# A decoder block's expert tiles go from 256 rows (15 tiles) to 128 rows (23 tiles)

## The reference

```python
gate_weights = softmax(x @ Wg + bg)            # 8 experts
topv, topi = top_k(gate_weights, 2)            # each token takes 2 of them
h = gelu(x @ W1[e] + b1[e])                    # 256 -> 512
h = gelu(h @ W2[e] + b2[e])                    # 512 -> 512
y = h @ W3[e] + b3[e]                          # 512 -> 256
out = sum over the token's two experts of topv * y
```

## Time and profile before

| | |
|---|---|
| time, median of 3 runs | 884.95 us (883.24 to 885.09) |
| span of the profiled execution | 896.7 us |
| mean granted TensorE clock | 0.855 of full speed |
| PE busy | 671.8 us (75%) |
| DVE busy | 527.2 us (59%) |
| ACT busy | 344.6 us (38%) |
| POOL busy | 317.1 us (35%) |

### The profile page before, as it was taken

One profiled execution on the slowest core, in us unless ns is written; L12 is line 12 of the kernel. 1 busy time (PEld: TensorE's weight loads), 2 busy tenths in 40 slices (PEclk: granted clock), 3 DMA queues, 4 the chain that ended last, 5 costly groups with the idle time before them and its releaser, 6 DMA issues.

```text
span 896.7 us, 12741 instructions
## 1 busy us (share of the span) xinstructions
PE 671.8 (75%) x3876; PEld 471.4 (53%) x3878; DVE 527.2 (59%) x1035; ACT 344.6 (38%) x967; POOL 317.1 (35%) x271
## 2 busy tenths in 40 slices
PE   4729895341999999955799999998867574977465
PEld 3327442330788888954535555566545353555233
DVE  4885999664455555515314434355587858467785
ACT  2403301422333333322335455466445241544544
POOL 2450587554000000024078465471156928110000
PEclk9959998555999999985599999999989766687787
DMA  9740002556411111144000000000120000000000
GB/s 332 261 141 0 1 0 94 168 176 209 107 48 47 47 47 47 37 121 144 1 0 1 1 0 0 0 0 1 52 89 0 1 0 1 0 0 0 0 18 29
DMA packets 35713, 49.81 MB, mean 56 GB/s; under 512 B 3032, under 2 KB 26784, under 8 KB 35424
## 3 DMA queue, kind: packets, MB, share of 16 engines
q1 hardware_dynamic: 33152, 41.26, 14.5%
q0 software_dynamic: 2528, 8.13, 2.5%
HBM read 38.37 MB, written 11.01 MB: 55 GB/s over the span
## 4 chain that ended last, share of the span: by engine, by line
PE 60%; DVE 20%; ACT 8%; issue 5%; POOL 3%; DMA 2%; another core or an unknown queue 1%; SPq 0%; DVEq 0%; ACTq 0%; POOLq 0%
PE bank L1500 13%; PE bank L1513 4%; PE bank L1617 4%; PE bank L1616 3%; PE bank L1671 3%; PE bank L1803 3%; POOL sorted_rows L469 3%; PE bank L1638 2%; PE bank L1821 2%; ACT sm L689 2%; PE bank L1388 2%; DVE qk L902 2%; PE bank L1431 2%; PE bank L1432 2%; ACT s5m L773 2%
## 5 line engine op out<-in xcount | busy, mean ns | idle before, releaser
L644 ACT ACTIVATE hf<-bank,be 128x256 f32<-128x256 f32 x120 | 50.5, 472 | 86.3 <-PE bank L1500 72.3
L1500 PE MATMUL bank<-h,wsp 128*128 128x256 f16 x720 | 81.3, 273 | 2.1 <-DVE h L1054 1.4
L475 POOL DMA_INDIRECT yg<-expert_rows,pos x16 | 15.6, 975 | 185.7 <-DMA expert_rows<-yb 181.1
L1500 PEld LDWEIGHTS bank<-h,wsp 128*128 x720 | 69.6, 98 | 12.0 <-issue 3.8
L773 ACT ACTIVATE s5m<-bank,n 128x128 f32<-128x128 f32 x128 | 45.4, 370 | 75.4 <-DVE n L1252 75.3
L1052 DVE CAST h<-hf 128x512 f16<-128x512 f32 x60 | 25.6, 427 | 65.1 <-ACT hf L644 63.6
L1803 PE MATMUL bank<-kx,q5s 128*128 128x512 f32 x64 | 43.7, 784 | 21.7 <-DVE q5s L1247 21.7
L457 POOL TENSOR_TENSOR kvp<-xnT,cxT 128x512 f32<-128x512 f32 x32 | 34.8, 1110 | 47.6 <-DVE xnT L881 39.6
L1157 DVE SCALAR_TENSOR_TENSOR sm<-bank,const 128x512 f32<-128x512 f32 x32 | 22.1, 691 | 50.1 <-PE bank L1638 50.1
L485 POOL TENSOR_TENSOR rq<-qs,const 128x256 f32<-128x256 f32 x32 | 23.2, 726 | 78.3 <-ACT qs L695 78.2
L559 ACT CAST wsp<-wraw 128x2048 f16<-128x2048 f32 x12 | 22.6, 1899 | 73.1 <-DMA wraw<-in_L_ffn_W 73.1
(11 more groups left out here) (300 smaller groups left out, 1631.1 us busy)
## 6 DMA issues: line engine op xcount, KB each, us to landing
wraw<-in_L_ffn_W SPq DMA_DIRECT2D x16, 512.0 KB, 4.5
wraw<-in_L_ffn_W SPq DMA_DIRECT2D x8, 1024.0 KB, 5.4
sorted_rows<-early POOLq DMA_DIRECT2D x2, 1920.0 KB, 14.0
xg<-sorted_rows SPq DMA_DIRECT2D x15, 256.0 KB, 2.8
expert_rows<-yb SPq DMA_DIRECT2D x15, 256.0 KB, 2.2
tapR<-in_kpad SPq DMA_DIRECT2D x16, 128.0 KB, 6.7
x<-in_x SPq DMA_DIRECT2D x1, 1024.0 KB, 5.9
cx<-in_ctx SPq DMA_DIRECT2D x1, 1024.0 KB, 10.0
```

What stands on the lines that cost most here:

```text
L644: last = nc.scalar.activation(hf[:, p, SLOTS * k:SLOTS * k + SLOTS], bank[2 * (layer - 1) + p][:, SLOTS * k:SLOTS * k + SLOTS], ACT.Gelu, ...
L1500: last = nc.tensor.matmul(b[:, SLOTS * (f % 2):SLOTS * (f % 2) + SLOTS], w[a_][:, c, P * f:P * f + P], inp[:, b_, c, :], start=(c == 0 and ...
```

## The change

`SLOTS` becomes 128, so `ET` becomes 2048/128 + 7 = 23, and a new `NB` = `SLOTS // P` = 1 takes the place of the number 2 wherever a tile consisted of two blocks of 128 rows. `turn_rows` has 2 transposes instead of 4, each matmul of layers 1 and 2 has 128 moving columns instead of 256, `layer3` has 12 matmuls instead of 24. The number of matmuls in layers 1 and 2 of a tile stays 72. The hardware loop makes ET//2 - 1 = 10 passes instead of 6; three tiles stay written out. The zero fill covers 2944 rows instead of 3840, and the table of expert numbers grows from 16 to 23 entries. The diff, with the renamed shapes of buffers left out:

```diff
-SLOTS = 2 * P
+SLOTS = P
+NB = SLOTS // P
 ET = 2 * NT * P // SLOTS + NE - 1
...
-        xg = sb("xg", [P, 2, 2, D], F32, sx)
+        xg = sb("xg", [P, 2, NB, D], F32, sx)
...
-            for k in range(2):
-                rows = ET * P
-                pool.dma_start(xs[rows * k:rows * k + rows, :].rearrange("(b p) d -> p b d", p=P), zeros).then_inc(sem("zero_filled"), 16)
+            for lo, hi in ((0, 12), (12, ET)):
+                pool.dma_start(xs[P * lo:P * hi, :].rearrange("(b p) d -> p b d", p=P), zeros[:, 0:hi - lo, :]).then_inc(sem("zero_filled"), 16)
...
-                nc.scalar.copy(yb[:, u].rearrange("p b d -> p (b d)"), bank[4 + u][:]).then_inc(sem("y_ready"), 1)
+                nc.scalar.copy(yb[:, u].rearrange("p b d -> p (b d)"), bank[4 + u][:, 0:NB * D]).then_inc(sem("y_ready"), 1)
...
-            then(nc.vector.tensor_tensor(eidg[:], cst["iota"].unsqueeze(2).to_broadcast([P, 16, NE - 1]),
-                                         tl[:, 1, 0:NE - 1].unsqueeze(1).to_broadcast([P, 16, NE - 1]), ALU.is_ge))
+            then(nc.vector.tensor_tensor(eidg[:], cst["iota"].unsqueeze(2).to_broadcast([P, ET, NE - 1]),
+                                         tl[:, 1, 0:NE - 1].unsqueeze(1).to_broadcast([P, ET, NE - 1]), ALU.is_ge))
...
-                nc.vector.tensor_copy(xgT[:, u, 0].rearrange("p c n -> p (c n)"), bank[6][:]).then_inc(sem("xgT_hi"), 1)
+                nc.vector.tensor_copy(xgT[:, u, 0].rearrange("p c n -> p (c n)"), bank[6][:, 0:DC * SLOTS]).then_inc(sem("xgT_hi"), 1)
...
-                    for b in range(2):
+                    for b in range(NB):
                         last = nc.tensor.transpose(bank[6][:, SLOTS * c + P * b:SLOTS * c + P * b + P], xg[:, u, b, P * c:P * c + P], ident)
...
-                for b in range(2):
+                for b in range(NB):
                     for c in range(FC):
                         if b == 0:
                             pe.wait_ge(sem("h2_lo"), i * 4 + (2 * u + c // 2 + 1 + CREDIT))
```

More of the change, by code:

```diff
@@ L71, in shape_constants @@
     parts["head16"] = np.kron(np.eye(8), np.ones((16, 1))) * 0.25
-    parts["iota"] = np.tile(np.arange(16.0), (P, 1))
+    parts["iota"] = np.tile(np.arange(float(ET)), (P, 1))
     parts["before"] = np.tile(np.tril(np.ones((NE, NE))).reshape(1, -1), (P, 1))
@@ L144, in decoder_kernel @@
         pos = sb("pos", [P, 2, NT], U32)
-        eidg = sb("eidg", [P, 16, NE - 1], F32)
-        eidf = sb("eidf", [P, 16], F32)
-        eid = sb("eid", [P, 16], I32)
+        eidg = sb("eidg", [P, ET, NE - 1], F32)
+        eidf = sb("eidf", [P, ET], F32)
+        eid = sb("eid", [P, ET], I32)
         comb = sb("comb", [P, NT, NE], F32)
@@ L158, in decoder_kernel @@
         sx = ExitStack()
-        xg = sb("xg", [P, 2, 2, D], F32, sx)
+        xg = sb("xg", [P, 2, NB, D], F32, sx)
         xgT = sb("xgT", [P, 2, 2, DC, SLOTS], F16, sx)
-        yb = sb("yb", [P, 2, 2, D], F32, sx)
+        yb = sb("yb", [P, 2, NB, D], F32, sx)
         hf = sb("hf", [P, 2, 2 * SLOTS], F32, sx)
@@ L424, in _ @@
             unused = early[:, NE // 2 - 1].rearrange("p a n -> p (a n)").bitcast(F32)
-            zeros = unused[:, 0:ET * D].rearrange("p (b d) -> p b d", d=D)
+            zeros = unused.rearrange("p (b d) -> p b d", d=D)
             nc.gpsimd.memset(unused, 0.0).then_inc(sem("zeroed"), 1)
@@ L1040, in split_rows @@
                 dve.wait_ge(sem("xgT_psum"), i * 2 + (u + 1))
-                nc.vector.tensor_copy(xgT[:, u, 0].rearrange("p c n -> p (c n)"), bank[6][:]).then_inc(sem("xgT_hi"), 1)
+                nc.vector.tensor_copy(xgT[:, u, 0].rearrange("p c n -> p (c n)"), bank[6][:, 0:DC * SLOTS]).then_inc(sem("xgT_hi"), 1)
                 dve.wait_ge(sem("xgT_hi"), i * 2 + (u + 1))
-                nc.vector.tensor_tensor(xgT[:, u, 1].rearrange("p c n -> p (c n)"), bank[6][:], xgT[:, u, 0].rearrange("p c n -> p (c n)"),
+                nc.vector.tensor_tensor(xgT[:, u, 1].rearrange("p c n -> p (c n)"), bank[6][:, 0:DC * SLOTS], xgT[:, u, 0].rearrange("p c n -> p (c n)"),
                                         ALU.subtract).then_inc(sem("xgT_split"), 1)
```

## The result

The changed kernel takes 940.85 us (median of 4 runs, 935.43 to 949.3); the kernel before, on the same chip, 885.02 (883.24 to 886.83). The ratio is 1.0625, 95% interval 1.0552 to 1.0698: slower by 56 us. The forecast was 938 us, with 908 to 960 as its range.

The account below looks back on a forecast made before the run. The prediction took the array as just full before and PE's sequencer as the bound after: 896.7 span + 60 (stage) - 1.4 (way in) = 955, less 12 and 5 for the profile, 938 us; range 908 to 960.

Parts of the forecast that it names:

- The bound: Layers 1 and 2: PE's sequencer, at 0.13 us a register instruction, limits the kernel once matmuls have 128 columns.
- A pass: One pass of the tile loop, two 128-row tiles, takes 20.0 us of sequencer time, 10.0 a tile.
- a pair of readings: Reading two expert numbers on PE's sequencer between tiles: 1.5 us, independent of the rows in a tile.
- What was taken off the old pass: From the old 22.2 us pass: 1.0 waiting in layer 3, 1.0 for 24 layer 3 matmuls, 0.2 for `turn_rows` transposes.
- The stage: All tiles: 4.1 us first tile, 200 us for ten passes, 26 us last three; 230 against 169.7, 60 more.
- The way in: Before the first tile: halved DVE operations, two transposes fewer and a smaller load save 1.4 us.
- The array's part: Matmuls of one 128-row tile need 5.6 us of array time, well under the sequencer's 10.0.
- From span to time: Whole kernel: 955 us span, less 12 us the profile adds, less 5 us as the new stage's share, gives 938.
- The falling clock: Rival: with the array waiting, the clock drops to 1.2 GHz, stage 16 us more, 956 us; chance 0.10.
- A new wait: Rival: a chain across engines comes late in each tile, about 0.6 us a tile, 952 us; chance 0.04.
- The lighter sequencer: Rival: without the profile a register instruction costs 0.11 us instead of 0.13, 912 us; chance 0.12.
- the array as the bound: Rival: the array sets the pace, a tile costs 5.6 us, 847 us in all; chance 0.04.

Follow-up runs that it names:

- The two experiments with fixed addresses: PE takes expert 0 or 1 instead of reading the number: changed 128-row kernel 846.84 us (ratio 0.9514), 256-row kernel before 885.22 us (0.9983).
- the step from two to three instructions a block: Changed kernel with the middle matmul of each block reading weights at its own address: 1014.66 us, ratio 1.14; a pass 25.74 us instead of 19.62.
- kernels with and without these matmuls: 256-row kernel before and 128-row changed kernel, each with a third register instruction a block: 912.29 and 1014.66 us, passes 25.84 and 25.74 us.
- s128_fixed: Changed 128-row kernel with PE taking expert 0 or 1, no expert number read, no weight address computed: 846.84 us, ratio 0.9514.
- the second profile of before: The kernel before, unchanged, profiled again: 887.52 us, span 885.7.

## Why the prediction was right, step by step

- **The bound** was named rightly: the sequencer's register instructions, found in rows that no busy share contains. The two experiments with fixed addresses show it, and the step from two to three instructions a block gives the price.
- **A pass** was put at 20.0 us; it is 19.62. The price of an instruction was right (0.13 us against 0.128), and so nearly was that of a pair of readings (1.5 us against 1.3 to 1.4). What was taken off the old pass, 2.2 us in all, had nearly the right sum under wrong names: 1.0 for waiting and 1.2 for 24 matmuls and four transposes that fall away. With three instructions a block, kernels with and without these matmuls differ by 0.1 us a pass, so nearly all of it was waiting (2.4 us a pass, as worked out above). That the sum came out so well owes something to luck: the prediction read a wait for the array as a price.
- **The stage** was put at 230 us and takes 224.7 (first matmul of layer 1 at 222.4, end of layer 3 at 447.1 where the last begins at 446.8). Four of the five us too many are the ten passes, the rest the way from layer 1 of the first tile to the loop. The last three tiles took 26 us, as put.
- **The way in**: -1.4 us. From the start of the last scatter to the first matmul it was 9.3 us and is 7.7, so -1.6.
- **The array's part** of 5.6 us a tile is what `s128_fixed` measures.
- **From span to time** the step was wrong. The 11.75 us were not a cost of the profile that a stage bound by the sequencer would share; they sat in one place of one execution. The changed kernel's profiled execution took 941.44 us with a span of 939.6, 1.8 apart. Taking 12 us off was right for a reason that I hadn't; the further 5 us were not there, and they made up for the 5 that the stage had too many. That 938 comes so near 940.85 is in part luck. The sum by what is known now, beside the second profile of before: the stage 54.5 us more (224.7 against 170.2), the way in 1.5 less, 0.9 more in the rest, which makes the spans 53.9 apart (939.6 and 885.7). The medians are 56 apart, and the changed kernel's own runs spread over 14.
- **The falling clock** was a rival at 956 us. It came true in short stretches: the stage has a mean of 0.95, and one pass 0.91 while the next has 1.00:

```profile
222.40:446.90 224.50, 189.39 (x1974) 150.46 (x1974) 84.36 (x227) 74.52 (x251) 0.00 (x0) 0.95 0.11 35
285.90:305.50 19.60, 16.52 (x172) 13.72 (x172) 7.45 (x20) 6.53 (x22) 0.00 (x0) 0.91 0.08 27
305.50:324.00 18.50, 16.34 (x172) 12.70 (x172) 7.03 (x19) 6.33 (x21) 0.00 (x0) 1.00 0.08 23
...
L1525 PEldq COMPARE_BRANCH  x3: 215/215/220, 283.9 to 323.0; - x3
```

It cost nothing that shows: the three branches of these two passes lie at 283.9, 303.5 and 323.0, 19.6 and 19.5 us apart. The rival needed the half clock all through the stage, where the array's 10.7 us a tile would be more than the sequencer's 10.0. Short stretches of it are covered by the 4.2 us a tile that the array has to spare (9.8 less 5.6).
- **A new wait** did not appear; ACT and DVE are at 33% and 38% in a pass. **The lighter sequencer** and **the array as the bound** are refuted.
